# A windowed-attention and expert kernel: in odd steps, the order of three TensorE products and of one VectorE pair is changed

## The reference, cut to what matters

```python
# x: (2, 2048, 256); 16 heads of 16; windows of 128 tokens; every 32nd token is "global"
q, k, v = x @ wq.T + bq, x @ wk.T + bk, x @ wv.T + bv
scores  = block-diagonal by window (q.k * scale), zero elsewhere,
          plus q.k * scale between the 64 global tokens of a batch
attn    = softmax(scores) @ v @ wo.T + bo
x       = layernorm(x + attn)
# expert part: top-1 of 8 experts by x @ Wg.T, each: layernorm -> scale/bias -> 256x64 -> gelu -> 64x256
x       = layernorm(x + expert(x))
```

## Time and profile before

| | |
|---|---|
| median of three runs | 443.73 us (443.46 to 445.12) |
| profiled execution | 447.08 us, span 445.3 us |
| TensorE busy | 407.0 us, 91% of the span |
| TensorE weight loads | 341.4 us, 77% |
| VectorE | 326.7 us, 73% |
| ScalarE | 251.0 us, 56% |
| GpSimd | 218.8 us, 49% |
| chain that ended last | PE 53%, DVE 27%, issue 8%, ACT 8%; the largest single line is `row_max`, 10% |
| mean granted clock of TensorE | 0.984 |

### The profile page before, as it was taken

One profiled execution on the slowest core, in us unless ns is written; L12 is line 12 of the kernel. 1 busy time (PEld: TensorE's weight loads), 2 busy tenths in 40 slices (PEclk: granted clock), 3 DMA queues, 4 the chain that ended last, 5 costly groups with the idle time before them and its releaser, 6 DMA issues.

```text
span 445.3 us, 14658 instructions
## 1 busy us (share of the span) xinstructions
PE 407.0 (91%) x5747; PEld 341.4 (77%) x5747; DVE 326.7 (73%) x797; ACT 251.0 (56%) x523; POOL 218.8 (49%) x300
## 2 busy tenths in 40 slices
PE   4889798999999999999999899988799998999991
PEld 3848687878888888888888788766577887777891
DVE  6695688757767767767769888563648998899785
ACT  2415575576576576576576567577554565554421
POOL 4341253455455455455455656536723585477540
PEclk9999999999999999999999999999979999999996
DMA  8562650100000000000020000000000011011004
GB/s 249 168 206 84 206 193 5 26 26 0 24 24 0 24 24 0 24 24 0 24 71 4 25 2 3 3 1 2 0 2 2 1 49 47 0 47 49 31 18 144
DMA packets 21721, 20.35 MB, mean 46 GB/s; under 512 B 3133, under 2 KB 21682, under 8 KB 21682
## 3 DMA queue, kind: packets, MB, share of 16 engines
q1 hardware_dynamic: 16900, 15.07, 10.7%
q10 hardware_dynamic: 4782, 4.75, 3.3%
HBM read 15.41 MB, written 4.41 MB: 45 GB/s over the span
## 4 chain that ended last, share of the span: by engine, by line
PE 53%; DVE 27%; issue 8%; ACT 8%; DMA 1%; ACTq 1%; DVEq 0%; POOL 0%; POOLq 0%
DVE row_max_t L1149 10%; PE ps L1456 8%; PE ps L1732 7%; PE ps L1419 7%; PE ps L1557 5%; PE ps L1379 5%; PE ps L1410 5%; PE ps L1433 3%; PE ps L1439 3%; ACT probs L841 2%; DVE k_part L1007 2%; PE ps L1401 2%; ACT boundsT_t L852 2%; ACT k_part L707 2%; PE ps L1423 2%
## 5 line engine op out<-in xcount | busy, mean ns | idle before, releaser
L841 ACT ACTIVATE probs<-ps 128x1024 f32<-128x1024 f32 x64 | 62.1, 1022 | 68.2 <-PE ps L1423 68.2
L1149 DVE TENSOR_REDUCE row_max_t<-ps 128x16 f32<-128x2048 f32 x31 | 70.9, 2288 | 3.8 <-PE ps L1410 3.6
L1732 PE MATMUL ps<-w_part,hm_part 128*128 128x256 f32 x384 | 54.5, 292 | 1.8 <-DVE hm_part L1327 1.8
L1410 PE MATMUL ps<-k_part,q_part 32*128 32x128 f32 x1584 | 51.5, 274 | 3.1 <-issue 1.3
L1410 PEld LDWEIGHTS ps<-k_part,q_part 32*128 32x128 f32 x1584 | 46.9, 186 | 9.2 <-issue 7.0
L1557 PE MATMUL ps<-xh_parts,w_part 128*128 128x512 f32 x192 | 53.7, 416 | 0.0
L557 POOL TENSOR_TENSOR q_part<-qf,q_part 128x512 fp32r<-128x512 f32 x32 | 41.0, 1283 | 25.7 <-ACT q_part L689 25.7
L1732 PEld LDWEIGHTS ps<-w_part,hm_part 128*128 128x128 f32 x384 | 48.9, 193 | 4.7 <-DVE hm_part L1327 2.4
L599 POOL TENSOR_TENSOR attn_t<-num_t,rden_t 128x256 f32<-128x256 f32 x32 | 20.0, 626 | 65.2 <-DVE rden_t L1180 65.2
L782 ACT ACTIVATE ffn_rows<-ps,b1s 128x512 f32<-128x512 f32 x32 | 22.0, 688 | 42.7 <-PE ps L1557 34.6
L1557 PEld LDWEIGHTS ps<-xh_parts,w_part 128*128 128x128 f32 x192 | 34.7, 194 | 6.5 <-issue 0.6
(11 more groups left out here) (233 smaller groups left out, 908.2 us busy)
## 6 DMA issues: line engine op xcount, KB each, us to landing
table<-rest_sums SPq DMA_DIRECT2D x4, 1088.0 KB, 6.8
xs<-in_L_attn_x_dram SPq DMA_DIRECT2D x16, 256.0 KB, 2.7
rows<-in_L_attn_x_dram ACTq DMA_DIRECT2D x4, 1024.0 KB, 7.7
out_dram<-yout SPq DMA_DIRECT2D x6, 512.0 KB, 2.9
w<-in_L_ffn_W_dram SPq DMA_DIRECT2D x2, 256.0 KB, 8.3
w<-in_L_ffn_W_dram SPq DMA_DIRECT2D x1, 512.0 KB, 3.9
out_dram<-yout SPq DMA_DIRECT2D x2, 256.0 KB, 2.6
out_dram<-yout ACTq DMA_DIRECT2D x2, 256.0 KB, 2.8
```

Of the source, the lines that this page charges most:

```text
L841: act.activation(probs[:, 2 * h:2 * h + 2, :], ps[:, 2 * h:2 * h + 2, :], ACT.Exp).then_inc(probs_ready, 1)
L1149: dve.tensor_reduce(row_max[:], ps_all, op=ALU.max, axis=AX.X).then_inc(max_ready, 1)
L1410: last = mm(ps[:, u, (2 * c + a) * P:(2 * c + a + 1) * P], q_part[x][quad(u), s, c, a, :], k_part[y][quad(u), s, c, :], start=(i == 0), st ...
L1732: mm(y, hm_part[a][:, 1 - p, f, c * P:(c + 1) * P], w2_part[b][:, f, :], start=(f == 0 and i == 0), stop=False)
```

## The change

It touches VectorE's and TensorE's steps of the attention loop, in odd steps only. No instruction is added or removed.

```diff
 # VectorE
                 if ahead and p == 0:
                     low_of_x(t + AHEAD)
-                if live(t + 1, steady) and p:
-                    keys_of(t + 1, (s + 1) % SLOTS)
...
                 early(1)
                 if ahead and p == 0:
                     queries_of(t + AHEAD)
+                if live(t + 1, steady) and p:
+                    keys_of(t + 1, (s + 1) % SLOTS)
                 early(2)
 # TensorE
+                soon = p and (steady or t < NW)
...
-                if live(t + 1, steady) and p:
-                    values_of(t + 1)
+                if old and soon:
+                    output_product(t - 3)
                 if live(t + 3, steady) and p:
                     turn_x(t + 3)
...
                 if pp:
                     pe.wait_ge(pvT_ready, t - 1)
                     turn_sums().then_inc(sums_in_psum, 1)
-                if old:
+                if old and not soon:
                     output_product(t - 3)
+                if live(t + 1, steady) and p:
+                    values_of(t + 1)
+                    second_values()
...
                 if ahead and p == 0:
                     keys_of(t + AHEAD)
-                if live(t + 1, steady) and p:
-                    second_values()
```

## The result

The changed kernel took 449.32 us (median of five runs, 447.47 to 449.83), the kernel before 443.73 us (443.46 to 445.58). The ratio, taken over runs on the same chip, is 1.0077 with a 95% interval of 1.0046 to 1.0107: slower by 3.4 us (2.0 to 4.7 us). The forecast was 445.2 us with a range of 442.4 to 447.2 us. By the ratio the changed kernel is at 447.1 us, the top edge of the range; its own median lies above it. The direction was right, the forecast size was less than half of what came. Counted by the prediction's own half per cent this is "slower", to which it gave a chance of 0.29. The two profiled executions are closer to each other than the medians are: spans of 445.3 and 445.6 us, both with a mean clock of 0.984. In both TensorE's clock falls to half at the same place, behind the thin stretch at 318 us.

The account below looks back on a forecast made before the run. TensorE's work was taken to bound the kernel. Terms -0.7 + 1.8 - 0.8 - 0.3 + 1.5 = +1.5 us on 443.73 us gave 445.2 us, range 442.4 to 447.2 us.

Parts of the forecast that it names:

- What bounds the kernel: Hardware loop: TensorE's work sets the pace, busy 32.72 of 33.40 us per four steps, leaving 0.68 us for reordering.
- The output product under the maximum: Loop: the product takes nearly the time of the six value MATMULs that leave its place; cost 0.
- The keys' low part behind the guards: Odd loop steps: the maximum starts 0.07 us earlier in each of ten steps, -0.7 us.
- the comparison of 0.12 us with the 0.05 us: Scores' end to maximum, odd step against start of a pass: the keys' low part costs the maximum 0.07 us.
- All the values ahead of the turned guards: Mid-pass even steps and step 24: `boundsT` comes 0.30 us later and delays the maximum, six times, +1.8 us.
- the tie: Mid-pass even step: x's low part ends at 151.71, scores at 151.68, maximum starts at 151.74, so it has no slack.
- From there VectorE goes without a pause to `num`: Mid-pass even step: VectorE is busy from maximum to `num`, so delaying x's low part delays the whole step.
- Step 1, -0.8 us: First step: six MATMULs leave the front of the turned scores, so exponentials and step 2's scores start earlier, -0.8 us.
- Steps 25 to 29, -0.3 us: Steps 25, 27 and 29: 0.07 us gained each, plus some of VectorE's 0.88 us in step 25; estimate -0.3 us.
- Step 31, +1.5 us: Output product ahead of the logits waits for `aT`; turned scores start 1.6 us late and delay `weigh` of step 32, +1.5 us.
- was not on this chain: Step 31: the product's absence behind `turn_sums` does not affect the chain from exponentials through `boundsT` to `weigh`.
- the clock as a rival: Fall at 322 us comes in most changed runs, few before: up to 3.35 us more, 448.6 us; chance 0.05.

Follow-up runs that it names:

- the best: Kernel before plus 22 extra turnings in step 35 and the change in steps 1 to 30, one window's values behind the guards, step 27's keys early: 442.52 us.
- TensorE's side alone: Changed kernel with 22 extra turnings in step 35, step 31 as before, and VectorE's keys' low part back ahead of the maximum: 443.75 us.
- the kernel with only step 31 changed: Kernel before plus 22 extra turnings in step 35, with step 31's output product moved ahead of the logits: 447.55 us, ratio 1.0062.
- the filled changed kernel: Changed kernel plus 22 extra identity turnings on TensorE in step 35's idle stretch: 446.91 us, ratio 1.0058 to the kernel before.

## Why the prediction was right or wrong

The forecast of +1.5 us agrees with the +1.4 us that the traces add up to without the clock, and that is luck: two terms of the loop were off by +0.7 and by -1.6 us, two small ones by 0.5 and 0.3 us, and the errors cancel. The clock then adds what brings the measured time to the edge of the range. The 443.5 and 446.8 us that the prediction calls its own bounds follow from no sum in it; the upper bounds of its terms add up to +5.0 us, 448.7 us.

**What bounds the kernel** was right. Four steps of the loop (12 to 16) stay at 33.4 us whatever the order: 33.41 to 33.43 in three traces of the kernel before, 33.41 to 33.45 in three of the changed one, 33.39 in the best. TensorE's work sets them. It was the reason for a small forecast.

**The output product under the maximum** in the loop costs nothing, as said: 0.20 us of load idle time are left ahead of the turned scores, where it was 0.35.

**The keys' low part behind the guards, -0.7 us in the loop**, failed: 0. The pair does fit behind the guards, but with it ahead of the maximum the intervals are the same. The step that failed is the comparison of 0.12 us with the 0.05 us of an even step: what released the maximum in the odd step was the scores too. Of the two sizes that this sets side by side, the odd step's stays as it is (0.12 and 0.13 us) when the pair is gone from in front of it.

**All the values ahead of the turned guards, +1.8 us**, was right up to the maximum and failed behind it. `boundsT` is 0.30 us late, to the hundredth, and the low part of x with it. The maximum of mid-pass even steps is late by 0.19 us. The missing 0.11 us was room in front of it: the two instructions start 0.72 us apart before (151.02, 151.74) and 0.60 us apart in the changed kernel (149.99, 150.59), so the tie read from the earlier trace rows was none. Behind the maximum the failing step is "From there VectorE goes without a pause to `num`". Before, these are the rows of step 14:

```profile
151.61 0.81 PEld L1433 LDWEIGHTS ps<-probs,va 128*32 128x32 f32 x32
...
154.25 0.42 PEld L1419 LDWEIGHTS ps<-q_part,k_part 32*128 32x128 f32 x12
...
154.55 1.66 DVE L998 SCALAR_TENSOR_TENSOR qf<-ps,vecT,q_scale 128x256 f32<-128x256 f32 x4
...
155.40 0.42 PEld L1439 LDWEIGHTS ps<-ident,pvT_t 128*128 128x128 f32 x4
...
156.27 0.44 DVE L1177 TENSOR_TENSOR num_t<-ps,rest_t 128x272 f32<-128x272 f32 x1
```

The queries (154.55 + 1.66 = 156.21 us) seem to run straight into `num` at 156.27. But `num` also waits for `turn_sums`, which began at 155.40, 0.87 us ahead of it. In the changed kernel it is 154.97 - 154.08 = 0.89 us, while the queries start 0.19 us later against `weigh` and `num` only 1.57 us behind them, not 1.72. So what seemed one busy chain had about 0.15 us of room. The turned scores too had 0.2 us: the maximum ended at 154.03, they began at 154.25. Counted on TensorE, nothing is left of the lateness: the turned scores start 2.64 us after `weigh` before and 2.66 us in the changed kernel, and from `weigh` of step 13 to that of 14 it is 7.95 us in both, from 14 to 15 8.56 and 8.58 us. The +0.18 us of one step and the -0.17 us of the next are those of VectorE's maximum alone. Both loop terms together were +1.1 us by forecast and +0.2 us by the trace, of which 0.1 us is the late maximum at the end of the stretch.

**Step 1, -0.8 us**, was right in kind: the scores of step 2 wait for the exponentials 0.54 us, where it was 1.27 us on the load's row. Step 1 itself gives -0.6 us. The stretch gives -0.8 us because step 3 adds -0.3 us, for which the prediction had no term.

**Steps 25 to 29, -0.3 us**, were wrong in sign: +0.2 us. Up to the maximum of step 25, 0.44 us are won. But 0.29 us of it are lost up to that of step 26, where `boundsT` is late and step 27 does not give it back, and 0.36 us up to that of step 28: in step 27 VectorE's setup work makes VectorE the bound, and the keys' low part moved from one side of the maximum to the other and so into the stretch that is bound. The kernel with TensorE's side alone and the best one, which have it at its old place in step 27, have 8.06 and 8.07 us there, not 8.43.

**Step 31, +1.5 us**, was right as a mechanism and as a size (1.5 to 1.8 us by the traces, 1.9 to 2.1 us by the runs of one group at equal clock), and wrong in what follows from it. I said that the product "was not on this chain". Its absence behind `turn_sums` opens a hole in TensorE's work, and in the kernel with only step 31 changed the clock fell there in one of two traces, at a cost of 2.95 us. Six of its ten runs, and six of the twelve of the filled changed kernel, are as slow and at as low a mean clock; that they fell at the same place is likely and not shown. The forecast had the clock as a rival with 0.05, at 322 us.

What the clock did in the changed kernel without the fill, whose 3.4 us are the result, stays open in part. With the fill the order costs 1.9 us at equal clock, and six of twelve runs pay 2.8 us more. Without it both traced runs of the changed kernel fell behind 322 us, as in that rival, and neither fell at 303 us. Ten of its 14 runs are below 0.990, and 48 of the 90 runs of before. So that rival may have had a share in the loss.

**The rule on the clock.** The Trainium skill, "TensorE: Matmul & The Clock Gate", section "Part 1: The HAM clock gate", has the gate watch activity without regard to the kernel's start. The runs fit this: the kernel with only step 31 changed has a mean clock of 0.988 or less in seven of eleven runs (six of ten, and the traced one) and 0.992 or 0.993 in the others, and its two traces have the same thin stretch, 2.20 and 2.21 us of work in 4, once with the fall and once without. That it is the gate's timing in which these runs differ, none of them shows.

## What to carry to other kernels

An order written for a loop has to be read once more in the steps before and behind the loop: there other work shares the engines, and a product that is free in twenty steps can wait in the one where its input is late. Where two chains seem tied, look at each instruction's other inputs before you call one of them the bound, since a busy engine without idle time can still have room. And on TensorE the place of filler matters twice, for the wait that it hides and for the clock behind it.

## What the runs showed of the hardware

A fall of TensorE's clock can cost as much as an order does, in a kernel whose TensorE is 91% busy. A half-level stretch of about 6.8 us (by the clocks 0.93, 0.50 and 0.95 of the three stretches from 299 to 312 us) in a busy part costs about 3 us (2.95 us between the two traces, and 445.73 against 448.57 us for the filled changed kernel), and 22 useless turnings in an idle stretch of 3 us make the time of the kernel before steadier: 443.31 to 445.14 us against 443.19 to 447.93 us. The share of runs below a mean clock of 0.990 differed between orders, from none of 12 to six of ten, and it has to be counted over several runs: one profiled execution of each kernel, with spans of 445.3 and 445.6 us, would have said that the change costs nothing.

Rows of one engine can overlap by a little. VectorE's `num` starts at 154.97 us in the changed kernel, and the row of the queries ahead of it ends at 153.40 + 1.66 = 155.06 us; before, it started at 156.27 behind an end at 156.21. So a start 0.06 us behind the last row's end does not show that the engine had no room.
